# Local attention: normalise the probabilities before their transpose, instead of the output after its product

## The reference, cut to what matters

```python
sim = jnp.einsum('bhwid,bhwjd->bhwij', bq, bk)
sim = jnp.where(mask, -jnp.finfo(sim.dtype).max, sim)
attn = jax.nn.softmax(sim, axis=-1)
out = jnp.einsum('bhwij,bhwjd->bhwid', attn, bv)
...
o = local_attention(q, k, v)
x = x + o @ wo
```

## Time and profile before

| | |
|---|---|
| median of 3 runs | 1874.72 us (1873.83 to 1874.86) |
| profiled execution | 1873.26 us |
| its span (first to last instruction) | 1871.5 us |
| mean granted TensorE clock | 0.997 |
| busy: PE, DVE, ACT, POOL | 1818.4, 1500.0, 1044.8, 440.4 us |

### The profile page before, as it was taken

One profiled execution on the slowest core, in us unless ns is written; L12 is line 12 of the kernel. 1 busy time (PEld: TensorE's weight loads), 2 busy tenths in 40 slices (PEclk: granted clock), 3 DMA queues, 4 the chain that ended last, 5 costly groups with the idle time before them and its releaser, 6 DMA issues. The chain is left out here.

```text
span 1871.5 us, 54122 instructions
## 1 busy us (share of the span) xinstructions
PE 1818.4 (97%) x20132; PEld 1595.0 (85%) x20132; DVE 1500.0 (80%) x4483; ACT 1044.8 (56%) x2487; POOL 440.4 (24%) x320
## 2 busy tenths in 40 slices
PE   8999999999999899999999999999999999989998
PEld 8779889889888788888888788878888888878887
DVE  6877877777777688998888777768888889877777
ACT  4443433433433388888887344437777777743333
POOL 0000000000000345455554000024455554501111
PEclk9999999999999999999999999999999999999999
DMA  9200000000010111111111200010111111110002
GB/s 336 65 1 2 1 1 2 1 1 2 1 71 2 56 28 27 28 25 28 26 27 34 92 12 12 11 46 22 26 27 27 25 28 27 32 34 7 12 11 96
DMA packets 66937, 61.42 MB, mean 33 GB/s; under 512 B 16479, under 2 KB 61323, under 8 KB 66830
## 3 DMA queue, kind: packets, MB, share of 16 engines
q1 hardware_dynamic: 66830, 59.93, 10.8%
HBM read 35.00 MB, written 8.39 MB: 23 GB/s over the span
## 5 line engine op out<-in xcount | busy, mean ns | idle before, releaser
L1156 ACT ACTIVATE l_probs<-l_probs,l_negmax 128x192 f32<-128x192 f32 x512 | 225.8, 442 | 104.9 <-DVE l_negmax L1269 104.9
L1114 POOL TENSOR_TENSOR l_t<-l_t,l_rnorm 128x512 f32<-128x512 f32 x128 | 138.8, 1106 | 261.4 <-DVE l_rnorm L1286 261.4
L1109 POOL TENSOR_TENSOR l_t<-l_t,l_t 128x1024 f32<-128x1024 f32 x64 | 152.5, 2382 | 126.7 <-DVE l_t L1321 126.7
L117 PE MATMUL ps<-local_w_hi,l_xT 128*128 128x512 f32 x384 | 157.9, 411 | 5.3 <-DVE l_xT L1229 2.0
L118 PE MATMUL ps<-local_w_lo,l_xT 128*128 128x512 f32 x384 | 151.0, 393 | 0.0
L119 PE MATMUL ps<-local_w_hi,l_xT 128*128 128x512 f32 x384 | 150.9, 393 | 0.0
L499 ACT ACTIVATE attn_exp<-ps 128x512 f32<-128x512 f32 x128 | 76.5, 600 | 116.9 <-PE ps L119 116.9
L117 PE MATMUL ps<-m_hnT_hi,ffn_w_hi 128*128 128x512 f32 (+1 forms) x352 | 141.0, 401 | 0.0
L118 PE MATMUL ps<-m_hnT_lo,ffn_w_hi 128*128 128x512 f32 (+1 forms) x352 | 138.4, 393 | 0.0
L119 PE MATMUL ps<-m_hnT_hi,ffn_w_lo 128*128 128x512 f32 (+1 forms) x352 | 138.3, 393 | 0.0
L1088 POOL MEMSET l_xT<- 128x520 f32 x2 | 1.1, 532 | 557.5 <-POOLq L463 555.6
(11 more groups left out here) (255 smaller groups left out, 6017.5 us busy)
## 6 DMA issues: line engine op xcount, KB each, us to landing
l_edge<-l_v SPq DMA_DIRECT2D x252, 64.0 KB, 2.0
tok_x<-x SPq DMA_DIRECT2D x16, 512.0 KB, 7.9
m_shifted<-shifted SPq DMA_DIRECT2D x20, 256.0 KB, 2.8
shifted<-x SPq DMA_DIRECT2D x64, 64.0 KB, 1.5
out<-x SPq DMA_DIRECT2D x8, 512.0 KB, 4.5
ffn_w_raw<-ffn_w SPq DMA_DIRECT2D x6, 640.0 KB
local_w_raw<-ffn_wqkv SPq DMA_DIRECT2D x4, 768.0 KB, 4.9
tok_base<-attn_base SPq DMA_DIRECT2D x4, 512.0 KB, 8.9
```

The costliest lines, as they stand in the source:

```text
L117: nc.tensor.matmul(out, wh, mh, start=start, stop=False, skip_group_check=True)
L1109: nc.gpsimd.tensor_tensor(t1[:], t1[:], t2[:], ALU.add).then_inc(s.summed.sem, 1)
L1114: nc.gpsimd.tensor_tensor(v, v, rn[:, a * LH:(a + 1) * LH].unsqueeze(2).to_broadcast([P, LH, DH]), ALU.mult).then_inc(s.rotated.sem, 1)
L1156: last = nc.scalar.activation(v, v, ACT.Exp, bias=nb[:, h:h + 1], scale=-1.0, accum_out=rsum[:, h:h + 1])
```

## The change

The probabilities are multiplied by the inverse of their row sums before they are transposed, so that the product with the values needs no scaling.

- **POOL**: the 128x512 spread of the inverses goes. In its place come two in-place products of the probabilities of four heads each (128x768) with the inverses, each counted by a new semaphore `normal`.
- **PE**: the four transposes of the spread inverses go. The twelve transposes of the probabilities move as one block behind the output product, the projection of the values and the transposes of x, ahead of the scores. They wait for `normal` (the first group for the first half, the others for the second). The scores' second half waits until ACT has copied two of the three groups, because these now use the scores' banks.
- **ACT**: the copy of the transposed inverses goes; the high part of the output is read from PSUM; the three copies of transposed probabilities move from ahead of the x copies to ahead of the exponentials.
- **DVE**: the product L1362 goes; the low part of the output is taken from PSUM and one SBUF tile instead of two SBUF tiles; the reciprocal waits for `normal` of the tile before.

```diff
-    XT, RB = 5, 6
-    PT = (XT, RB, TQ)
+    XT, PB = 5, 6
+    PT = (TQ, TQ + 1, PB)
...
-            def spread_out(t):
-
-                wait(pool, s.r_t, t)
+            def normalise(t):
+
                 pool.wait_ge(*s.inverted.after(t + 1))
-                wide = rinv[:].unsqueeze(2).to_broadcast([P, LH, DH])
-                nc.gpsimd.tensor_tensor(spread[:].rearrange("p (h d) -> p h d", d=DH), wide,
-                                        one[:].unsqueeze(2).to_broadcast([P, LH, DH]), ALU.mult).then_inc(s.spread.sem, 1)
+                for half in range(2):
+                    heads = slice(half * LH // 2, (half + 1) * LH // 2)
+                    v = pm[:].rearrange("p m (e k) -> p (m e) k", e=2)[:, heads]
+                    nc.gpsimd.tensor_tensor(v, v, rinv[:, heads].unsqueeze(2).to_broadcast([P, LH // 2, REACH]),
+                                            ALU.mult).then_inc(s.normal.sem, 1)
...
                 if d:
-                    wait(act, s.o_norm, n - 2)
+                    wait(act, s.o_full, n - 2)
                     wait(act, s.y_full, n - 3)
-                    nc.scalar.activation(oth[:], on[:], ACT.Copy).then_inc(s.o_hi.sem, 1)
+                    nc.scalar.activation(oth[:], ps[:, OT], ACT.Copy).then_inc(s.o_hi.sem, 1)
...
-                if c:
-                    for k in range(THIRDS):
-                        probs_out(n - 2, k)
...
                 if c:
-                    wait(act, s.r_t, n - 1)
-                    wait(act, s.o_done, n - 2)
-                    nc.scalar.activation(on[:], ps[:, RB], ACT.Copy).then_inc(s.r_out.sem, 1)
+                    for k in range(THIRDS):
+                        probs_out(n - 2, k)
...
-                    wait(dve, s.spread, n - 2)
+                    wait(dve, s.normal, 2 * (n - 2))
                     nc.vector.reciprocal(rinv[:], rsum[:]).then_inc(s.inverted.sem, 1)
...
-                    nc.vector.tensor_tensor(otl[:], on[:], f32(oth[:]), ALU.subtract).then_inc(s.o_done.sem, 1)
+                    nc.vector.tensor_tensor(otl[:], ps[:, OT], f32(oth[:]), ALU.subtract).then_inc(s.o_done.sem, 1)
...
-                if c:
-                    wait(dve, s.o_full, n - 1)
-                    wait(dve, s.r_out, n - 1)
-                    nc.vector.tensor_tensor(on[:], ps[:, OT], on[:], ALU.mult).then_inc(s.o_norm.sem, 1)
...
             def probs_t(t, k):
-                wait(pe, s.exped, 4 * t + k + 2)
+                wait(pe, s.normal, 2 * t + (2 if k else 1))
...
                 if c:
-                    wait(pe, s.spread, n - 1)
-                    wait(pe, s.p_done, THIRDS * (n - 1))
-                    inverses()
+                    if not b:
+                        wait(pe, s.masked, 4 * (n - 1))
+                    for k in range(THIRDS):
+                        probs_t(n - 2, k)
                 if b:
                     score(0, 1 - r)
+                    if c:
+                        wait(pe, s.p_done, THIRDS * (n - 2) + 2)
+                        pe.sem_inc(s.banks_free.sem, 1)
                     score(1, 1 - r)
                 if c:
+                    wait(pe, s.p_done, THIRDS * (n - 1))
                     wait(pe, s.v_done, n - 1)
```

More of the change, by code:

```diff
@@ L981, in local_phase @@
     ms = K.mlp_s[layer]
-    (xc, xt, sq, t1, t2, qt, kt, vv, edge, pm, pt, on, spread, oth, otl), at = mem.place(
+    (xc, xt, sq, t1, t2, qt, kt, vv, edge, pm, pt, oth, otl), at = mem.place(
         K.mlp_end, mem.end, (f"l{layer}_x", [P, 2, D], F32),
@@ L989, in local_phase @@
         (f"l{layer}_probs", [P, LPAIRS, 2 * REACH], F32), (f"l{layer}_probsT", [P, 3 * LPAIRS, P], F32),
-        (f"l{layer}_oT", [P, LINNER], F32), (f"l{layer}_spread", [P, LINNER], F32), (f"l{layer}_oT_hi", [P, LINNER], F32R),
-        (f"l{layer}_oT_lo", [P, LINNER], F32R))
+        (f"l{layer}_oT_hi", [P, LINNER], F32R), (f"l{layer}_oT_lo", [P, LINNER], F32R))
     assert at <= K.mlp_small
-    (idle, one, ss, rn, tmp, nb, rsum, rinv), at = mem.place(
-        K.local_small, mem.end, (f"l{layer}_idle", [P, 1], F32), (f"l{layer}_one", [P, 1], F32),
+    (idle, ss, rn, tmp, nb, rsum, rinv), at = mem.place(
+        K.local_small, mem.end, (f"l{layer}_idle", [P, 1], F32),
         (f"l{layer}_ss", [P, 2 * LH], F32),
@@ L1126, in _ @@
             for t in (T - 2, T - 1):
-                spread_out(t)
+                normalise(t)
         @block.scalar
@@ L1463, in values @@
                 last.then_inc(s.o_full.sem, 1)
-            def inverses():
-                for pair in range(LPAIRS):
-                    last = nc.tensor.transpose(ps[:, RB, pair * P:(pair + 1) * P],
-                                               spread[:, pair * P:(pair + 1) * P],
-                                               K.ident[:])
-                last.then_inc(s.r_t.sem, 1)
             def step(n, r, a, b, c, d):
@@ L1496, in step @@
                     turned_t(n - 1, 0)
-                if c:
-                    probs_t(n - 2, 0)
-                if b:
                     turned_t(n - 1, 1)
-                if c:
-                    wait(pe, s.r_out, n - 2)
-                    probs_t(n - 2, 1)
-                if c:
-                    if b:
-                        wait(pe, s.qk_done, 2 * n - 1)
-                    else:
-                        wait(pe, s.masked, 4 * (n - 1))
-                    probs_t(n - 2, 2)
                 if drain(n, 1):
-                    keep_warm(nc, K, QK, 8)
+                    keep_warm(nc, K, XT, 8)
                 if drain(n, 2):
@@ L1524, in step @@
                 if a and not first:
-                    if c:
-                        wait(pe, s.p_done, THIRDS * (n - 2) + 1)
                     x_t(n + 1, 1 - r)
@@ L1944, in __init__ @@
         self.p_done = count("p_done")
-        self.r_t = count("r_t")
-        self.r_out = count("r_out")
-        self.spread = count("spread")
+        self.normal = count("normal")
         self.inverted = count("inverted")
@@ L1964, in __init__ @@
         self.y_full = count("y_full")
-        self.o_norm = count("o_norm")
+        self.banks_free = count("banks_free")
 class MlpCounts:
```

3 lines of the change are left out of this document (1 added, 2 removed).

## The result

The changed kernel takes 1877.74 us (median of 13 runs, 1871.63 to 1881.82); the kernel before takes 1873.94 in 13 runs on the same chip. The ratio is 1.0019, with a 95% interval of 1.0010 to 1.0027: slower by 0.19%, where 1868.5 and a gain of 0.3% were forecast. The time lies in the range, on the wrong side of no change.

What follows compares the result with a forecast made beforehand. PE was taken as the bound (pair 24.63 us), a POOL ring just below (24.11). A pair of 24.37 gains 0.26, over 28 pairs 7.3; drains cost 1: -6.3, thus 1867.0 profiled, 1868.5 median; range 1860 to 1886.

Steps and rivals of the forecast that it cites:

- the piece: POOL's 128x308 subtraction on weights, once per pair of steps: forecast to fall from 1.28 to 0.86 us without DVE's interference.
- The long step: Step with the piece of weights and the mask: forecast 12.47 us, decided by POOL, against 12.21 on the other path.
- POOL's ring: Waits from POOL's products through PE's transposes, DVE's rotation, POOL's addition and DVE's inverse norm back to the next products.
- the pair of the forecast: Long plus short step after the change: 24.37 us against 24.63 before, a gain of 0.26 in each of 28.
- floor of 24.11: Shortest pair of steps the ring of waits allows: 24.11 us, 0.52 below the 24.63 of the kernel before.
- PE, order: Probability transposes moved behind other PE work: POOL ready at 3.6 to 3.7 us, PE not waiting, some 0.4 to spare.
- the short step: Step without the piece and mask: forecast 11.90 us, as POOL's new products (2.83) fit within 3.35.
- The drains: Tiles finishing one behind the other at each layer's end: between -1 and +2 us a layer, taken as +0.5.
- the first steps: Steps outside the 28 pairs, such as a layer's first: near the ring's floor already, so no gain counted.
- Rival 1: POOL's new product costs the proportional 1.57 us: pair 24.59, gain eaten by drains, no change, 1874.7; chance 0.26.
- Rival 3: Another lock or wait: piece still 1.28 us (pair 24.79, 1880), or ACT's copies late for the values; chance 0.13.
- "Faster" with 0.46: Chance that the kernel gets faster: 0.36 for the forecast plus 0.10 for rival 4, normalising hidden whole (1861).

Runs made afterwards that it cites:

- experiment 6: Changed kernel plus one more POOL addition (128x308, scratch tile) behind the piece of weights, in 28 long steps: 1895.87 us, ratio 1.0120.
- experiment 7: Experiment 3's kernel plus one more POOL addition (128x308, scratch tile) behind the piece of weights, in 28 long steps: 1891.53 us, ratio 1.0094.
- experiment 11: Experiment 3's kernel with the piece of weights still on POOL, in two halves, one behind the products of each step: 1863.63 us, ratio 0.9954.
- experiment 1: Changed kernel with ACT's copy of the values moved ahead of its copies of q and k: 1869.92 us, ratio 0.9984.
- experiment 3: Changed kernel with both edits, ACT's values copy first and spare identity transposes where PE idled: 1868.51 us, ratio 0.9968.
- experiment 10: Kernel before the change with the piece of weights moved from POOL to DVE: 1874.28 us, ratio 0.9999.
- experiment 2: Changed kernel with spare identity transposes where PE idled, in the third step and first drain step, to keep the clock up: 1873.36 us, ratio 0.9996.
- experiment 8: Experiment 3's kernel with the piece of weights moved from POOL to DVE, at the head of each pair's second step: 1866.14 us, ratio 0.9955.
- experiment 9: Changed kernel with the piece of weights moved from POOL to DVE: 1877.63 us, ratio 1.0014.
- experiment 12: Changed kernel with the piece of weights on POOL in two halves, one behind the products of each step: 1878.31 us, ratio 1.0032.

## Why the prediction was wrong

**What held.** POOL's products (1.467 for 1.46), the piece (0.84 for 0.86) and the low part are as forecast. By the Trainium skill, "GPSIMD Engine Reference", section 3.1, the estimate was 1.69; the trace does not bear it out for a product with a broadcast operand. The long step (12.39 from products to products, for 12.47) is POOL's, and experiments 6, 7 and 11 show POOL's ring as a bound. Experiments 1 and 3 give the pair of the forecast, 24.33 and 24.44 for 24.37. Its floor of 24.11 is nearly reached in experiment 11, where POOL's work fits beside it: 24.14. The kernel before had POOL hidden (experiment 10).

**The step that failed is "PE, order".** It asked only when the probabilities' transposes themselves would find their data, and concluded that PE "waits for nothing there". But all twelve of them (1.41 us) had stood between the projection of k and that of the values, ahead of the wait for `v_done`. They had hidden ACT's squares and three copies. Moved behind, they leave that wait bare: 0.39 us in each of 60 steps, more than PE waits for POOL's products (11.3 us in 46), the only gaps that were forecast. What was asked was who waits for the moved block. What was not asked is who had been served by its length. The waits view of the kernel before has this wait with only two cases, of 0.5 us at most:

```profile
PEld ps L117 <- ACT l_v L1190: 1.1, 2, 0.5
```

**The mis-sized term** is thus the short step: 12.17 to 12.27 instead of 11.90, a pair of 24.55 instead of 24.37. With 28 pairs that is 5 us of the 7.3. Another 0.7 is the kernel before: the forecast took layer 0's pair of 24.63 for both layers, and layer 1's is 24.58.

**The drains** were taken at +0.5 a layer. With the clock up they cost 0.60 and 0.72 (experiment 2), as sized. With the clock down the first cost 1.75, and the third step 1.5 more. The forecast said that the first steps count nothing, and it had no term for the clock, though it made PE idle in stretches that had been filled. Experiment 2 gives back 4.4 us between medians, of which the traces show 2.7 at the places of its edit; with it the change makes no difference that can be told from the kernel before (0.9996, 0.9987 to 1.0005). Nor had the forecast a term for the second MLP, where the profiled execution loses 2.2 us. Whether the change has a part in that longer wait for a transfer is open.

**The rivals.** Rival 1 had nearly the right pair (24.59) for the wrong reason. Rival 3 named the right kind of mishap, a late copy by ACT, but the wrong reader of it: the values product waits for the probabilities' copies only twice, in all 2.2 us, and it is the projection that waits for the values copy. "Faster" with 0.46 hung on one ring, with no chance for a second one right below it. Before, PE's own 24.63 covered both.

**Open.** The steady pairs of layer 1 take 0.1 us longer than those of layer 0, in experiments 1, 3, 6, 7 and 11 alike. In experiment 3's trace this is POOL's idle time behind the addition of a long step, 4.29 us instead of 4.18; why, was not tried, nor was a shorter drain. The long wait for the transfer in the second MLP (2.8 to 3.4 us) stands in the profiled executions of the changed kernel and of experiments 1, 8, 9 and 12; in the others, and in the kernel before, it is 1.7 to 2.0. That the clock's drops differ from execution to execution rests on the changed kernel's 13 runs, where the mean granted clock was 0.997 in the two shortest (1871.63 and 1874.06) and 0.993 in the longest (1881.82), and on four profiles: in the changed kernel and in those of experiments 6, 9 and 12 the third step took 13.3 to 14.7 us in five of eight layers, and 11.9 in the other three.

## What to carry to other kernels

When a block of work is moved back in an engine's order, list every wait that stood behind it, not only its own: its length was cover for them, and the one whose slack was smallest is the new bound. When the binding engine is relieved by a few per cent, look for all rings just under it; here three lay within 2% (PE 24.63, PE with ACT 24.54, POOL 24.33), so that removing one was worth the distance to the next. And a relieved TensorE may idle at single places long enough to lose its clock; a few idle transposes there can be worth as much as the change.

## What the runs showed of the hardware

- Behind gaps of 1.01, 0.28 and 1.17 us in PE's work (646.7 to 650.4), and behind one of 2.21 us (ahead of 1030.09), the granted clock fell to its lower level, and 512 columns took 0.63 us instead of 0.40. The gaps alone don't decide it: in the same execution 1.02, 0.28 and 1.18 us in the third step of layer 1 and 2.22 us at its drain (ahead of 1655.03) left it at 1.00. With 18 idle transposes in the one place and 18 more in the other it stayed at 1.00 in both, in the profiled execution.
- The exclusion between POOL and a DVE instruction with two SBUF sources is paid by both. A 128x308 subtraction takes 0.99 us on DVE where POOL is busy (987 to 994 ns in all 28 cases, an estimated 0.43 alone), and POOL's two products take 0.24 more than with the mask alone. The Trainium skill, "SBUF — State Buffer", section "Who interferes with whom", says that such a DVE instruction contends with a GpSimd instruction that reads SBUF; the runs agree, also in the other direction: with PSUM as one source the low part takes 0.69 us in all 64 cases, 62 of them beside POOL's work.
- On POOL a product with a broadcast operand takes 1.467 us for 768 columns and 1.046 for 512, a contiguous operation 0.84 for 308 and 0.51 for 154: worked out from these pairs, a fixed part of about 0.2 us stands beside one for each column, 1.64 and 2.1 ns.
